# Whitening in place: output tiles written where their input tiles lay, and 26 instead of 21 tile places in SBUF

## The chip, the cores and the metric

One core of one Trainium2 chip. The time is that of one execution in device microseconds; of several executions the median is given. The profile is of one further execution. Engines are named TensorE (PE in the rows, its weight loads PEld), VectorE (DVE), ScalarE (ACT), GpSimd (POOL) and SyncE (SP), whose queue issues every DMA of this kernel. One core has 16 DMA engines.

## What is computed

Two layers on x of shape (4, 64, 256, 256), float32. First, each channel is convolved with a separable long filter (causal in both directions) and x times a bias is added. Then the result is whitened over channels:

```python
x1   = transpose(x, (1, 0, 2, 3)).reshape(64, -1)
x1_s = x1[:, ::9]                                   # every ninth position
mean = x1_s.mean(-1);  cov = x1_s @ x1_s.T / n + 0.01 * I
D    = isqrt_newton_schulz(cov, 5)                  # five Newton steps
out  = D @ (x1 - mean)                              # back to (4, 64, 256, 256)
```

The whole convolution must be done before the covariance is known, and the covariance before the first output.

## The kernel before

**Convolution.** 128 units (64 channels in each of two sweeps, two of the four images per sweep). For a unit, SP loads a tile of x (`x_sb`, five slots) and two Toeplitz tiles made from the filters (`hankel`), ScalarE and GpSimd split operands into a rounded high part and a rest (`rounded`), TensorE does two passes of matmuls (L633 to L636, `make_v`, `make_y`), VectorE adds bias times x into `y_sb` (L510, two slots), SP stores that to `y_dram` in HBM (`store_y`, two DMAs of 256 KB), GpSimd multiplies it by a mask of every ninth position into `masked` (L368), and VectorE sums that into `z_sb` (L518). TensorE is one unit ahead of the evictions.

**Join.** `z_sb` gives the covariance (`covariance`, 58 matmuls per sweep; that of the second sweep is what `cov_mm` 2 stands for). Then a chain of small operations between TensorE, VectorE and ScalarE makes `dmat` (the matrix D on 128 partitions, both image halves at once) and the mean's share in `small[:, 6:7]` (`d_ready`). Its small operands (`cov`, `sq`, `wm` and so on) lie in `z_all` behind the output slots, the constants `halves`, `ident15`, `ident_eps`, `twice` in the last x slot.

**Whitening.** 64 tiles of 128 x 2048 float32, 1 MB each (`TILES`, `TW`). A tile is loaded from `y_dram` to a place `t_in[t % slots]`, multiplied by `dmat` in four matmuls of 512 columns (L744; the profile has two records of each), the left half evicted from PSUM by ScalarE (L442) and the right half by VectorE (L613) into one of `O_SLOTS` = 4 output slots `t_out`, and stored to `out` (L287). ScalarE and VectorE wait until the store of tile t - 4 has landed. There are 21 places: 14 (`kept`) are loaded during the second sweep, three lie in `rounded`, one in `plain`, two in `x_all`, one in `y_all`; `z_all` and `masked_all` hold the output slots.

SP's queue is one order written out by hand. After the last unit: loads of tiles 14 to 17 (when TensorE has done its last convolution matmul, `y_mm`), `store_y(LAST)`, tiles 18 and 19, a wait for all stores of y (L299) and for the last masks and sums (`z_last_done`), tile 20. Then per tile t:

```python
while loaded < min(TILES, max(slots + t * 2 // 5, t + LEAD)):   # LEAD = 7
    sp.wait_ge(t_mm[1], loaded - slots + 1)                     # its place has been read
    load_tile(loaded)
    loaded += 1
sp.wait_ge(t_act, t + 1)
sp.wait_ge(t_dve, t + 1)                                        # L313
store_tile(t)
```

So two loads go out for every five tiles, until the lead of the loads has come down to 7 tiles; from then on one load per tile.

Of the kernel before, what the change touches and what calls it, by code (L numbers as in the profile page):

```python
# [13 lines left out]
P = 128  # L14
# [43 lines left out]
O_SLOTS = 4  # L58
# [4 lines left out]
def conv_whiten(nc, x, first, hidden, columns, bias, out):  # L63
# [3 lines left out]
    with ExitStack() as ctx:  # L67
# [8 lines left out]
        kept = sb("kept", [P, KEPT * TW])  # L76
# [13 lines left out]
        plain = sb("plain", [P, T_SLOTS * 2 * P + 2 * 2 * S + H_SLOTS * 2 * S])  # L90
# [7 lines left out]
        x_all = sb("x_all", [P, X_SLOTS * XW])  # L98
        x_sb = [x_all[:, k * XW:(k + 1) * XW] for k in range(X_SLOTS)]
        y_all = sb("y_all", [P, 2 * XW])  # L100
        y_sb = [y_all[:, k * XW:(k + 1) * XW] for k in range(2)]
        masked_all = sb("masked_all", [P, 2 * BLOCKS * GW])
        masked = [masked_all[:, k * BLOCKS * GW:(k + 1) * BLOCKS * GW].rearrange("p (i w) -> p i w", w=GW)
                  for k in range(2)]
        z_all = sb("z_all", [P, ZROWS * ZW])
        z_sb = z_all[:, :].rearrange("p (r m) -> p r m", m=ZW)
# [16 lines left out]

        o_cols = (O_SLOTS - 1) * TW
        cov, sq, t_even, t_odd, dmat, wm, mm_sq, zm = (z_all[:, o_cols + k * P:o_cols + (k + 1) * P] for k in range(8))
        tm = (t_even, t_odd)
        ident15, ident_eps, halves, twice = (x_sb[X_SLOTS - 1][:, k * P:(k + 1) * P] for k in range(4))

        t_in = [kept[:, k * TW:(k + 1) * TW] for k in range(KEPT)]
        t_in += [rounded[:, k * TW:(k + 1) * TW].bitcast(F32) for k in range(3)] + [plain[:, 0:TW]]  # L130
        after_v = len(t_in)
        t_in += [x_all[:, k * TW:(k + 1) * TW] for k in range(2)]
        after_y = len(t_in)
        t_in += [y_all[:, 0:TW]]
        slots = len(t_in)
        t_out = [z_all[:, k * TW:(k + 1) * TW] for k in range(O_SLOTS - 1)] + [masked_all[:, 0:TW]]

# [27 lines left out]
        t_loaded = [sem(f"t_loaded{k}") for k in range(slots)]  # L165
        t_mm = [sem(f"t_mm{u}") for u in range(2)]
        t_act, t_dve = sem("t_act"), sem("t_dve")
        t_stored = [sem(f"t_stored{k}") for k in range(O_SLOTS)]
# [32 lines left out]
        def _(sp):  # L201
# [81 lines left out]
            def load_tile(t):  # L283
                sp.dma_start(t_in[t % slots], tile_in(t, 0, TW)).then_inc(t_loaded[t % slots], 16)

            def store_tile(t):
                sp.dma_start(out[t], t_out[t % O_SLOTS]).then_inc(t_stored[t % O_SLOTS], 16)  # L287


            sp.wait_ge(y_mm, UNITS)  # L290
            for t in range(KEPT, after_v):
                load_tile(t)
            store_y(LAST)
            for t in range(after_v, after_y):
                load_tile(t)
            for k in range(2):
                sp.wait_ge(y_stored[k], 32 * (UNITS // 2))
            sp.wait_ge(masked_half, PER)
            sp.wait_ge(z_last_done, 2 * PER)  # L299
            for t in range(after_y, slots):  # L300
                load_tile(t)
# [476 lines left out]
```

## Time and profile before

| | |
|---|---|
| three runs | 954.18, 952.86, 945.55 us, median 952.86 |
| profiled execution | 948.63 us, span 946.5 us |
| granted TensorE clock, mean | 0.996 |
| busy: TensorE, weight loads, VectorE, ScalarE, GpSimd | 868.5, 729.9, 576.3, 401.0, 494.5 us |
| DMA | 306.36 MB, mean 324 GB/s |

The span runs from the first to the last instruction of the profiled execution; the execution's own time is 2.1 us longer. All times in the rows are microseconds from the start of the span, unless they are marked ns. The busy share of an engine over the whole span is an average over the three stages above; they have to be read apart.

### The profile page before, as it was taken

The page shows a single profiled execution, that of the slowest core. Times are in us where ns is not written, and L with a number is a line of the kernel's source. Part 1 is how long each engine was busy: PE and PEld are TensorE (multiplying, and loading weights), DVE is VectorE, ACT ScalarE, POOL GpSimd, SP SyncE. Part 2 cuts the span into 40 slices and gives each one's busy share as a digit, 9 for nine tenths or more (in the row PEclk, how much of TensorE's full clock was granted, in tenths as well). Part 3 has the DMA queues.
Part 4 walks back from the last instruction along what each step waited for, and adds up shares of the span by engine and source line. Part 5 has one row for each costly group of instructions (what it writes and reads, how often), then busy time and mean ns, then how long its engine had stood idle before and what let it go on. Part 6 is the DMA issues. An engine that isn't in the chain of part 4 may idle for free.

```text
span 946.5 us, 15709 instructions
## 1 busy us (share of the span) xinstructions
PE 868.5 (92%) x5970; PEld 729.9 (77%) x5970; DVE 576.3 (61%) x641; ACT 401.0 (42%) x715; POOL 494.5 (52%) x278
## 2 busy tenths in 40 slices
PE   2799999999999999999999999999999997777774
PEld 0799999999999999999999999999544442322221
DVE  5388787788888847878777878784333332222222
ACT  2355555555555525555555555550233322222221
POOL 2298888888888856878777778771000000000000
PEclk9999999999999999999999999999999999999998
DMA  2799998999999866999999999988499999999998
GB/s 105 218 315 293 284 283 276 297 278 291 279 287 287 283 218 194 341 335 339 329 343 332 357 334 330 340 279 331 170 413 422 421 423 427 427 427 427 427 428 360
DMA packets 99351, 306.36 MB, mean 324 GB/s; under 512 B 13484, under 2 KB 48333, under 8 KB 84685
## 3 DMA queue, kind: packets, MB, share of 16 engines
q1 hardware_dynamic: 99276, 305.37, 90.8%
q8 instruction: 47, 0.77, 0.3%
q14 instruction: 28, 0.22, 0.1%
HBM read 167.96 MB, written 137.36 MB: 323 GB/s over the span
## 4 chain that ended last, share of the span: by engine, by line
PE 77%; DMA 18%; DVE 3%; issue 1%; ACT 0%; SPq 0%; DVEq 0%; ACTq 0%
PE ps L636 24%; DMA out<-z_all 17%; PE ps L633 13%; PE ps L634 13%; PE ps L635 13%; PE ps L744 10%; PE ps L665 3%; DVE z_all L613 1%; DVE kept L470 1%; PE ps L684 0%; DMA plain<-filters 0%; PE ps L624 0%; ACT z_all L442 0%; DMA kept<-hidden 0%; PE ps L721 0%
## 5 line engine op out<-in xcount | busy, mean ns | idle before, releaser
L633 PE MATMUL ps<-rounded 128*128 128x256 f32 x1024 | 373.7, 365 | 10.3 <-DVE rounded L499 8.7
L368 POOL TENSOR_TENSOR masked_all<-y_all,mask 128x1024 f32<-128x1024 f32 x126 | 326.3, 2590 | 63.3 <-DVE y_all L510 63.1
L635 PE MATMUL ps<-rounded 128*128 128x256 f32 x1024 | 289.5, 283 | 0.0
L634 PE MATMUL ps<-rounded 128*128 128x256 f32 x1024 | 288.4, 282 | 0.0
L510 DVE SCALAR_TENSOR_TENSOR y_all<-x_all,bias_sb,ps 128x1024 f32<-128x1024 f32 x127 | 162.5, 1280 | 96.8 <-DMA convolved<-y_all 60.5
L334 POOL TENSOR_TENSOR rounded<-x_all,rounded 128x512 fp32r<-128x512 f32 x128 | 165.1, 1290 | 83.1 <-ACT rounded L401 82.5
L633 PEld LDWEIGHTS ps<-rounded 128*128 128x128 f32 x1024 | 196.5, 192 | 11.8 <-issue 11.4
L636 PE MATMUL ps<-plain,x_all 128*128 128x128 f32 x1024 | 197.4, 274 | 0.0
L634 PEld LDWEIGHTS ps<-rounded 128*128 128x128 f32 x1024 | 197.3, 193 | 0.0
L636 PE MATMUL ps<-plain 128*128 128x128 f32 x1024 | 196.4, 273 | 0.0
L635 PEld LDWEIGHTS ps<-rounded 128*128 128x128 f32 x1024 | 192.9, 188 | 0.0
L744 PE MATMUL ps<-kept,z_all 128*128 128x512 f32 x344 | 152.3, 596 | 22.2 <-ACT z_all L442 17.2
L636 PEld LDWEIGHTS ps<-plain,x_all 128*128 128x128 f32 x1024 | 159.0, 191 | 0.0
L636 PEld LDWEIGHTS ps<-plain 128*128 128x128 f32 x1024 | 158.0, 190 | 0.0
L518 DVE TENSOR_REDUCE z_all<-masked_all 128x116 f32<-128x1044 f32 x126 | 155.5, 1234 | 0.0
L744 PEld LDWEIGHTS ps<-kept,z_all 128*128 128x128 f32 x344 | 63.8, 190 | 109.7 <-issue 109.7
L613 DVE TENSOR_SCALAR z_all<-ps,small 128x1024 f32<-128x1024 f32 x48 | 61.6, 1284 | 140.6 <-PE ps L744 75.4
L408 ACT COPY plain<-ps 128x512 f32<-128x512 f32 x128 | 75.0, 586 | 156.1 <-PE ps L636 155.7
L442 ACT ACTIVATE z_all<-ps,small 128x1024 f32<-128x1024 f32 x48 | 53.4, 1113 | 157.2 <-DMA out<-z_all 102.9
L401 ACT CAST rounded<-x_all 128x512 fp32r<-128x512 f32 x128 | 80.2, 626 | 77.4 <-DMA x_all<-x 77.0
L490 DVE TENSOR_TENSOR rounded<-ps,rounded 128x512 fp32r<-128x512 f32 x128 | 87.9, 686 | 28.1 <-ACT rounded L410 27.9
L499 DVE TENSOR_TENSOR rounded<-plain,rounded 128x512 fp32r<-128x512 f32 x128 | 90.7, 709 | 13.4 <-ACT rounded L392 13.4
(103 smaller groups left out, 479.8 us busy)
## 6 DMA issues: line engine op xcount, KB each, us to landing
x_all<-x SPq DMA_DIRECT2D x128, 512.0 KB, 5.6
convolved<-y_all SPq DMA_DIRECT2D x256, 256.0 KB, 5.3
out<-z_all SPq DMA_DIRECT2D x48, 1024.0 KB, 15.7
plain<-filters SPq DMA_DIRECT2D x256, 128.0 KB, 4.8
kept<-convolved SPq DMA_DIRECT2D x29, 1024.0 KB, 19.9
out<-masked_all SPq DMA_DIRECT2D x16, 1024.0 KB, 15.2
kept<-convolved SPq DMA_DIRECT2D x28, 512.0 KB, 6.3
rounded<-convolved SPq DMA_DIRECT2D x9, 1024.0 KB, 20.2
```

Of the source, the lines that this page charges most:

```text
L334: nc.gpsimd.tensor_tensor(x_lo[k], row_block(q % X_SLOTS, 0), x_hi[k].bitcast(F32), ALU.subtract).then_inc(x_lo_done, 1)
L368: nc.gpsimd.tensor_tensor(masked_of(k, 0, PER), by_image(y_sb[k]), mask_of(q // C, 0, PER), ALU.mult).then_inc(masked_done, 1)
L401: nc.scalar.copy(x_hi[q % 2], row_block(k, 0)).then_inc(x_hi_done, 1)
L490: nc.vector.tensor_tensor(v_lo[k], ps_v[k][:, :, 0:S], v_hi[k].bitcast(F32), ALU.subtract).then_inc(v_lo_done, 1)
L499: nc.vector.tensor_tensor(t_lo[k], hankel[h][:, :, ::-1], t_hi[k].bitcast(F32), ALU.subtract).then_inc(t_lo_done, 1)
L510: nc.vector.scalar_tensor_tensor(y_sb[k], x_sb[q % X_SLOTS], bias_sb[:, q % C:q % C + 1], ps_y[k].rearrange("p a n -> p (a n)"), ALU.mult, ...
L518: nc.vector.tensor_reduce(z_of(q % C), grouped(q % 2, 0, BLOCKS), AX_X, ALU.add).then_inc(z_done, 1)
L633: mm(wide, hi[:, b, cols], t_hi[k][:, f, :], start=True, stop=False)
L634: mm(wide, hi[:, b, cols], t_lo[k][:, f, :], start=False, stop=False)
L635: mm(wide, lo[:, b, cols], t_hi[k][:, f, :], start=False, stop=False)
L636: last = mm(o[:, b, m * S + P:(m + 1) * S], block1[:, b, cols], t_f32[k][:, f, :], start=False, stop=True)
L744: last = mm(ps[:, bank(t, u) + r, :], dmat, t_in[k][:, w:w + IMG], start=True, stop=True)
```

## The change

All buffers of the convolution that are float32 now lie in one tensor `arena` of 24 tile widths: `kept`, `plain`, `x_all`, `y_all`, `z_all`, `masked_all`, in this order and without gaps. Whitening sees the same stretch as 23 places of one tile each, and three more in `rounded`, which are only read. The 24th tile width holds the small operands of the join. A tile's output is written where its input lay, half by half, once the matmuls of that half are done; the tiles in `rounded` (14, 15 and 16) write to the places of tiles 7, 8 and 9, whose stores they wait for. Output slots are gone. A load waits until the store of the tile that had its place has landed (it waited for matmuls before). Place and waits of every tile are worked out ahead, from a queue `free`.

SP's order after the last unit: tiles 14 to 18, `store_y(LAST)`, tiles 19 and 20, the wait for all stores of y and for the last masks, tile 21, waits for `z_last_done` and now also `cov_mm` 2, tiles 22 to 25. The loop then has 26 where it had 21. `halves` is set after a wait of GpSimd for `z_last_done`.

```diff
--- before.py
+++ after.py
@@ -55,7 +55,11 @@
 TILES = SWEEPS * SWEEP_TILES
 KEPT = 14
 PIECES = 2
-O_SLOTS = 4
+ARENA = 24 * TW
+READ_ONLY = 3
+OUT_OF = 7
 LEAD = 7
 MASK_COLS = 288
@@ -73,7 +77,14 @@
-        kept = sb("kept", [P, KEPT * TW])
+        arena = sb("arena", [P, ARENA])
+        taken = [0]
+        def region(cols):
+            taken[0] += cols
+            return arena[:, taken[0] - cols:taken[0]]
+        kept = region(KEPT * TW)
         rounded = sb("rounded", [P, 14 * 2 * S], F32R)
@@ -87,7 +98,7 @@
         v_hi = [rounded_at(10 + k, S) for k in range(2)]
         v_lo = [rounded_at(12 + k, S) for k in range(2)]
-        plain = sb("plain", [P, T_SLOTS * 2 * P + 2 * 2 * S + H_SLOTS * 2 * S])
+        plain = region(T_SLOTS * 2 * P + 2 * 2 * S + H_SLOTS * 2 * S)
         t_f32 = [plain[:, k * 2 * P:(k + 1) * 2 * P].rearrange("p (f n) -> p f n", n=P) for k in range(T_SLOTS)]
         at = T_SLOTS * 2 * P
         v_f32 = [plain[:, at + k * 2 * S:at + (k + 1) * 2 * S].rearrange("p (f n) -> p f n", n=S) for k in range(2)]
@@ -95,15 +106,15 @@
         hankel = [plain[:, at + k * 2 * S:at + (k + 1) * 2 * S].rearrange("p (f n) -> p f n", n=S)
                   for k in range(H_SLOTS)]
-        x_all = sb("x_all", [P, X_SLOTS * XW])
+        x_all = region(X_SLOTS * XW)
         x_sb = [x_all[:, k * XW:(k + 1) * XW] for k in range(X_SLOTS)]
-        y_all = sb("y_all", [P, 2 * XW])
+        y_all = region(2 * XW)
         y_sb = [y_all[:, k * XW:(k + 1) * XW] for k in range(2)]
-        masked_all = sb("masked_all", [P, 2 * BLOCKS * GW])
+        z_all = region(ZROWS * ZW)
+        z_sb = z_all[:, :].rearrange("p (r m) -> p r m", m=ZW)
+        masked_all = region(2 * BLOCKS * GW)
         masked = [masked_all[:, k * BLOCKS * GW:(k + 1) * BLOCKS * GW].rearrange("p (i w) -> p i w", w=GW)
                   for k in range(2)]
-        z_all = sb("z_all", [P, ZROWS * ZW])
-        z_sb = z_all[:, :].rearrange("p (r m) -> p r m", m=ZW)
         mask = sb("mask", [P, MASK_COLS])
@@ -121,19 +132,37 @@
         index, idx, near = (kept[:, 12 * S + k * MASK_COLS:12 * S + (k + 1) * MASK_COLS] for k in range(3))
-        o_cols = (O_SLOTS - 1) * TW
-        cov, sq, t_even, t_odd, dmat, wm, mm_sq, zm = (z_all[:, o_cols + k * P:o_cols + (k + 1) * P] for k in range(8))
+        in_place = ARENA // TW - 1
+        places = [arena[:, k * TW:(k + 1) * TW] for k in range(in_place)]
+        places += [rounded[:, k * TW:(k + 1) * TW].bitcast(F32) for k in range(READ_ONLY)]
+        resident = len(places)
+        after_v, after_x, after_y = KEPT + 2, KEPT + 4, KEPT + 5
+        in_at = [*range(KEPT), *range(in_place, resident), *range(KEPT, in_place)]
+        out_at, stores_of = [], [0] * in_place
+        stores_before_load, stores_before_out = [0] * resident, []
+        loads_of, loads_before = [0] * resident, []
+        free = []
+        for t in range(TILES):
+            if t >= resident:
+                in_at.append(free.pop(0))
+                stores_before_load.append(stores_of[in_at[t]])
+            k = in_at[t]
+            loads_of[k] += 1 if t >= KEPT else 0
+            loads_before.append(loads_of[k])
+            out_at.append(k if k < in_place else OUT_OF + k - in_place)
+            stores_before_out.append(0 if k < in_place else stores_of[out_at[t]])
+            stores_of[out_at[t]] += 1
+            if not OUT_OF <= t < OUT_OF + READ_ONLY:
+                free.append(out_at[t])
+        behind = [arena[:, in_place * TW + k * P:in_place * TW + (k + 1) * P] for k in range(TW // P)]
+        cov, sq, t_even, t_odd, dmat, wm, mm_sq, zm = behind[:8]
+        halves, ident15, ident_eps, twice = behind[12:]
         tm = (t_even, t_odd)
-        ident15, ident_eps, halves, twice = (x_sb[X_SLOTS - 1][:, k * P:(k + 1) * P] for k in range(4))
-        t_in = [kept[:, k * TW:(k + 1) * TW] for k in range(KEPT)]
-        t_in += [rounded[:, k * TW:(k + 1) * TW].bitcast(F32) for k in range(3)] + [plain[:, 0:TW]]
-        after_v = len(t_in)
-        t_in += [x_all[:, k * TW:(k + 1) * TW] for k in range(2)]
-        after_y = len(t_in)
-        t_in += [y_all[:, 0:TW]]
-        slots = len(t_in)
-        t_out = [z_all[:, k * TW:(k + 1) * TW] for k in range(O_SLOTS - 1)] + [masked_all[:, 0:TW]]
         ps = ctx.enter_context(nc.psum_tensor("ps", [P, 8, S * 2], F32))
         ps_v = [ps[:, 2 * k:2 * k + 2, :] for k in range(2)]
@@ -162,10 +191,10 @@
         t_ready, sq_mm, sq_copied = sem("t_ready"), sem("sq_mm"), sem("sq_copied")
         w_mm, w_copied, z_mm, z_copied = sem("w_mm"), sem("w_copied"), sem("z_mm"), sem("z_copied")
         d_made, mean_mm, d_ready = sem("d_made"), sem("mean_mm"), sem("d_ready")
-        t_loaded = [sem(f"t_loaded{k}") for k in range(slots)]
+        t_loaded = [sem(f"t_loaded{k}") for k in range(resident)]
-        t_stored = [sem(f"t_stored{k}") for k in range(O_SLOTS)]
+        t_stored = [sem(f"t_stored{k}") for k in range(in_place)]
         def wait(eng, s, value):
             if value > 0:
@@ -281,39 +310,42 @@
                 load_kept(q)
             def load_tile(t):
-                sp.dma_start(t_in[t % slots], tile_in(t, 0, TW)).then_inc(t_loaded[t % slots], 16)
+                wait(sp, t_stored[out_at[t]], 16 * stores_before_load[t])
+                sp.dma_start(places[in_at[t]], tile_in(t, 0, TW)).then_inc(t_loaded[in_at[t]], 16)
             def store_tile(t):
-                sp.dma_start(out[t], t_out[t % O_SLOTS]).then_inc(t_stored[t % O_SLOTS], 16)
+                sp.dma_start(out[t], places[out_at[t]]).then_inc(t_stored[out_at[t]], 16)
             sp.wait_ge(y_mm, UNITS)
-            for t in range(KEPT, after_v):
+            for t in range(KEPT, after_v + READ_ONLY):
                 load_tile(t)
             store_y(LAST)
-            for t in range(after_v, after_y):
+            for t in range(after_v + READ_ONLY, after_x + READ_ONLY):
                 load_tile(t)
             for k in range(2):
                 sp.wait_ge(y_stored[k], 32 * (UNITS // 2))
             sp.wait_ge(masked_half, PER)
+            for t in range(after_x + READ_ONLY, after_y + READ_ONLY):
+                load_tile(t)
             sp.wait_ge(z_last_done, 2 * PER)
-            for t in range(after_y, slots):
+            sp.wait_ge(cov_mm, 2)
+            for t in range(after_y + READ_ONLY, resident):
                 load_tile(t)
-            loaded = slots
+            loaded = resident
             for t in range(TILES):
-                while loaded < min(TILES, max(slots + t * 2 // 5, t + LEAD)):
-                    sp.wait_ge(t_mm[1], loaded - slots + 1)
+                while loaded < min(TILES, max(resident + t * 2 // 5, t + LEAD)):
                     load_tile(loaded)
                     loaded += 1
                 sp.wait_ge(t_act, t + 1)
                 sp.wait_ge(t_dve, t + 1)
                 store_tile(t)
-            for k in range(O_SLOTS):
-                sp.wait_ge(t_stored[k], 16 * (TILES // O_SLOTS))
+            for k in range(in_place):
+                sp.wait_ge(t_stored[k], 16 * stores_of[k])
         @block.gpsimd
         def _(pool):
@@ -377,6 +409,7 @@
             chained(nc.gpsimd.tensor_scalar(ident_eps, ident[:], EPS, None, ALU.mult))
             for k in range(2):
                 nc.gpsimd.tensor_tensor(twice[:, k * C:(k + 1) * C], ident[:, 0:C], ident[:, C:P], ALU.add)
+            pool.wait_ge(z_last_done, 2 * PER)
             nc.gpsimd.memset(halves, 0.5).then_inc(ident_ready, 1)
         @block.scalar
@@ -437,9 +470,9 @@
             for t in range(TILES):
                 act.wait_ge(t_mm[0], t + 1)
-                wait(act, t_stored[t % O_SLOTS], 16 * (t // O_SLOTS))
+                wait(act, t_stored[out_at[t]], 16 * stores_before_out[t])
                 src = ps[:, bank(t, 0):bank(t, 0) + 2, :].rearrange("p r n -> p (r n)")
-                nc.scalar.activation(t_out[t % O_SLOTS][:, 0:TW // 2], src, ACT.Identity,
+                nc.scalar.activation(places[out_at[t]][:, 0:TW // 2], src, ACT.Identity,
                                      bias=small[:, 6:7]).then_inc(t_act, 1)
         @block.vector
@@ -608,9 +641,9 @@
             for t in range(TILES):
                 dve.wait_ge(t_mm[1], t + 1)
-                wait(dve, t_stored[t % O_SLOTS], 16 * (t // O_SLOTS))
+                wait(dve, t_stored[out_at[t]], 16 * stores_before_out[t])
                 src = ps[:, bank(t, 1):bank(t, 1) + 2, :].rearrange("p r n -> p (r n)")
-                nc.vector.tensor_scalar(t_out[t % O_SLOTS][:, TW // 2:TW], src, small[:, 6:7], None, ALU.add
+                nc.vector.tensor_scalar(places[out_at[t]][:, TW // 2:TW], src, small[:, 6:7], None, ALU.add
                                         ).then_inc(t_dve, 1)
         @block.tensor
@@ -730,9 +763,9 @@
             for t in range(TILES):
                 if t < KEPT:
                     pe.wait_ge(kept_loaded, 16 * KEPT * PIECES)
-                k = t % slots
-                wait(pe, t_loaded[k], 16 * (t // slots + (1 if k >= KEPT else 0)))
+                k = in_at[t]
+                wait(pe, t_loaded[k], 16 * loads_before[t])
                 if t == 1:
                     pe.wait_ge(d_ready, 1)
@@ -741,7 +774,7 @@
                     wait(pe, t_dve if u else t_act, t - 1)
                     for r in range(2):
                         w = (2 * u + r) * IMG
-                        last = mm(ps[:, bank(t, u) + r, :], dmat, t_in[k][:, w:w + IMG], start=True, stop=True)
+                        last = mm(ps[:, bank(t, u) + r, :], dmat, places[k][:, w:w + IMG], start=True, stop=True)
                     last.then_inc(t_mm[u], 1)
```

## Rows read from the trace of the kernel before

**Rows 1.** The page: 40 equal slices of the span, DMA share in tenths, bytes per second.

```profile
DMA  2799998999999866999999999988499999999998
GB/s 105 218 315 293 284 283 276 297 278 291 279 287 287 283 218 194 341 335 339 329 343 332 357 334 330 340 279 331 170 413 422 421 423 427 427 427 427 427 428 360
```

**Rows 2.** The chain that ended last, 640 to 946 us, longest pieces: start, length, what.

```profile
669.42 85.96 PE ps L744 x200
...
873.89 18.17 DMA out<-z_all
```

**Rows 3.** Waits, 664 to 946 us: engine line, released by: total us, times, longest.

```profile
ACT z_all L442 <- DMA out<-z_all: 102.9, 28, 3.8
...
DVE z_all L613 <- DMA out<-z_all: 65.1, 19, 3.6
...
ACT masked_all L442 <- DMA out<-masked_all: 34.6, 10, 3.8
...
DVE masked_all L613 <- DMA out<-masked_all: 21.7, 6, 3.6
```

**Rows 4.** Stretches: length, each engine, granted clock, DMA share, GB/s.

```profile
652.00:656.00 4.00, 4.00 (x38) 4.00 (x38) 0.00 (x0) 0.00 (x0) 0.00 (x0) 1.00 1.02 378
...
664.00:674.40 10.40, 10.08 (x46) 6.37 (x46) 4.09 (x12) 1.11 (x1) 0.00 (x0) 1.00 0.04 14
674.40:684.00 9.60, 9.60 (x24) 4.22 (x23) 3.27 (x3) 3.34 (x3) 0.00 (x0) 1.00 0.74 300
684.00:700.00 16.00, 16.00 (x39) 7.15 (x38) 5.72 (x5) 5.57 (x5) 0.00 (x0) 1.00 1.00 383
700.00:755.00 55.00, 55.00 (x130) 24.35 (x129) 20.54 (x16) 17.37 (x16) 0.00 (x0) 1.00 1.01 422
755.00:930.00 175.00, 136.80 (x303) 54.66 (x302) 47.51 (x37) 40.52 (x37) 0.00 (x0) 1.00 1.01 426
930.00:941.00 11.00, 5.08 (x12) 1.78 (x10) 3.85 (x3) 3.34 (x3) 0.00 (x0) 0.91 1.01 428
941.00:944.00 3.00, 0.00 (x0) 0.00 (x0) 0.00 (x0) 0.00 (x0) 0.00 (x0) 0.50 0.55 232
944.00:946.50 2.50, 0.00 (x0) 0.00 (x0) 0.00 (x0) 0.00 (x0) 0.00 (x0) 0.50 0.06 26
```

**Rows 5.** SP's queue in order of time: start, duration of the issues, DMAs.

```profile
641.19 2.12 SPq L284 DMA_DIRECT2D rounded<-convolved  x3
643.35 1.41 SPq L284 DMA_DIRECT2D plain<-convolved  x1
645.53 1.25 SPq L242 DMA_DIRECT2D convolved<-y_all  x2
646.83 1.06 SPq L284 DMA_DIRECT2D x_all<-convolved  x2
659.09 0.32 SPq L284 DMA_DIRECT2D y_all<-convolved  x1
674.43 7.13 SPq L287 DMA_DIRECT2D out<-z_all  x3
681.61 0.42 SPq L284 DMA_DIRECT2D kept<-convolved  x1
```

**Rows 6.** TensorE in order of time: the second covariance.

```profile
644.27 13.19 PE L665 MATMUL ps<-z_all 128*128 128x129 f32 x116 [1.14 <-DVE z_all L548]
```

**Rows 7.** GpSimd in order of time, inside the convolution (idle before in brackets).

```profile
301.75 2.77 POOL L368 TENSOR_TENSOR masked_all<-y_all,mask 128x1024 f32<-128x1024 f32 x1 [0.62 <-DVE y_all L510]
304.49 1.28 POOL L334 TENSOR_TENSOR rounded<-x_all,rounded 128x512 fp32r<-128x512 f32 x1
306.38 2.78 POOL L368 TENSOR_TENSOR masked_all<-y_all,mask 128x1024 f32<-128x1024 f32 x1 [0.62 <-DVE y_all L510]
```

**Rows 8.** DMA issues, 640 to 700, then 700 to 946 us: median us to landing.

```profile
out<-z_all SPq DMA_DIRECT2D x6, 1024.0 KB, 5.8
...
out<-z_all SPq DMA_DIRECT2D x42, 1024.0 KB, 18.1
```

## The prediction

> **What bounds the kernel now.** I read the page's 40 slices first. The DMA row is at 9 nearly everywhere from the second slice on, falls to 4 in the slice from 662 to 686 us (the 29th) and is then 9 to the end, while GB/s goes from about 280 to 340 in the convolution to about 425 behind it [rows 1]. So there are three stages with different limits: the convolution (TensorE has no gap in it), a short join of covariance and Newton steps, and whitening. The chain of waits says what sets the end of the last: one piece of 86 us of TensorE (L744, 200 matmul records, 0.43 us each, so 3.43 us for the eight records of a tile), and from 755 us on stretches of 18.2 us of an output's transfer with one short eviction between them [rows 2]. The waits give the same from the other side: ScalarE waited 102.9 + 34.6 us and VectorE 65.1 + 21.7 us until an output tile had left its slot [rows 3]. That looks like a shortage of output slots, which is just what this change removes. The stretches show that it isn't one: from 755 to 930 us the DMA engines are at 1.01 and move 426 GB/s, no less than anywhere else in the trace [rows 4]. A slot comes free late because the transfers before it fill all sixteen engines. In whitening the time is the number of bytes divided by 426 GB/s, plus the time in which those engines stand still.
>
> They stand still once: 0.04 busy from 664.0 to 674.4 and 0.74 from 674.4 to 684.0, so 10.0 + 2.5 = 12.5 us idle [rows 4]. SP's queue says why. After the last matmul of the convolution it issues four loads, the last unit's two stores, two more loads, one at 659.09, and then nothing until the first output at 674.43: all 21 places are taken [rows 5].
>
> **The change part by part.** *Bytes.* The same 64 tiles are loaded once and stored once, 1.0486 MB each; one such transfer is 1.0486 MB / 426 GB/s = 2.46 us. Nothing is removed from the bytes.
>
> *Five more loads ahead of the first output.* With 26 places instead of 21, five loads (5 x 2.46 = 12.3 us) go ahead of tile 0. When? Five (not four) are issued once the last matmul is done, then the last unit's stores, then two. The next waits for those stores. Before, they had landed at 659.09 [rows 5]; one load more stands ahead of them, so 661.5. The queue then still holds what it held before (it ran dry at 664 with the load of 659.09 in it, so at 661.5 without, plus 2.46 us for the fifth: 664.0), a margin of 2.5 us. The four last places need the second covariance as well (the new wait on cov_mm), whose matmuls end at 644.27 + 13.19 = 657.46 [rows 6]: earlier, so this wait ends nothing. The five loads thus run from 664.0 to 676.3, of which 10.4 us lie in the hole and 1.9 us run on past the first store's issue at 674.43. Stores come every 3.43 us there (three issues in 7.13 us [rows 5]) and take 2.46 us, so the hole's tail takes these up; but between second and third store some 0.8 us stay idle because the third isn't computed yet. Of 12.5 us idle, 12.5 - 0.8 = 11.7 us are filled.
>
> *Is a filled hole time saved?* Only if a queue stands behind it. Until the loads catch up, one store and 0.4 load per tile cost 1.4 x 2.46 = 3.44 us of DMA for 3.43 us of TensorE: balanced, no backlog, TensorE ends last. The loop goes over to one load per tile where 21 + 0.4t falls below t + 7, at t = 24 (751 us, and the chain turns to DMA at 755 [rows 2]); with 26 it is t = 32. So eight tiles, 27 us, move from the DMA-bound rate to the balanced one, which shows 422 instead of 426 GB/s [rows 4]: 0.3 us lost. Behind t = 32 the DMA has 4.92 us of work per tile against TensorE's 3.43, a backlog grows by 1.49 us a tile, and everything saved ahead of it is saved at the end: 11.7 - 0.3 = 11.4 us.
>
> *Waits of ScalarE and VectorE on output slots.* These 224 us of waiting vanish, since an output has its input's place; only tiles 14, 15 and 16 wait, for the stores of tiles 7, 8 and 9, issued 24 us earlier. Worth nothing by itself: what is late next is the load. LEAD is still 7, so once TensorE has run ahead it stops for the load of its own tile, behind about six loads and six stores, 12 x 2.46 = 29.5 us. Expect TensorE waiting for DMA where it waited for ScalarE. At the end the last load has some five stores queued behind it (12.3 us) and the last tiles need 3.43 + 1.3 us, so the DMA stays full. Before it was full there too: 1.01 up to 941, then 0.55 and 0.06 [rows 4], so nothing is won at the tail.
>
> *Load waits at the head of SP's queue.* The load of tile n now waits for the landed store of an earlier tile, where it waited for matmuls. The stores that follow stand behind it in that queue. The tight one is the first, load 26 at t = 3, which needs store 0. That one starts at 676.3, ends at 678.8; the first six outputs took 5.8 us to land (the median), with a short queue, which with 1.9 us for the spill is 682.1 [rows 8], against an SP that came there at 681.61 [rows 5]: about 0.5 us of waiting, with a store still in the queue. Next comes store 1 at t = 5, 3.4 us later relative to need, and from n = 33 on the distance is 23 to 24 tiles. I take zero. Upper bound: a store lands as late as 12.3 us after issue, as the last unit's two did (issued by 646.8, landed 659.09, with two loads behind them [rows 5]); SP would then stand until 686.7 and the fourth output go out 2 us late. Loss 2 to 5 us, no gain possible.
>
> *Small things.* `halves` now waits on GpSimd for z_last_done, ahead of 657.46, and is read after it: nothing. Of 23 final waits instead of four, at most 8 follow the last landing, 0.05 us each at the "issue" pieces' size: 0.2 us, taken as 0.2.
>
> *Layout of the convolution's buffers.* No instruction is added in 128 units. The trace can't show the new addresses. GpSimd is the engine with least room: product 2.78 us, difference 1.28 us, idle 0.62 us, in a unit of 4.63 us [rows 7]. The two products shown write different halves of masked_all, 4,176 bytes apart, and take 2.77 and 2.78 us; so I price another address at nothing. The Trainium skill (SBUF — State Buffer, Door 1: the DMA port swizzle) says that lines of SBUF are 16 bytes and each crossing to a new one costs; masked_all now begins at byte 186,600 of the stretch, 8 past such a line, one line more per row of 1,024 bytes. That would be at most 1 part in 64 of 2.78 us, 0.04 us, inside the idle; the sum is the same by it.
>
> Sum: 11.4 - 0.2 = 11.2 us off the profiled execution, 948.6 - 11.2 = 937.4 (span 946.5 to 935.3). The median of the three runs shown is 952.9 and gives 941.7; the three runs and the profiled one have a mean of 950.3 and give 939.1. I say 940.
>
> The Trainium skill speaks against the rate on which all this rests: DMA: Bandwidth & Descriptors (Where 436 GB/s comes from) has transfers between HBM and SBUF bound by some 358 GB/s per core. By it a transfer would take 2.93 us and five of them 14.6 us, 2.2 us more than the hole holds. The trace disagrees, with 426 GB/s over 175 us [rows 4].
>
> **The rivals.** *The deeper queue moves fewer bytes per second (slower).* Before, an output took 18.1 us to land [rows 8], so 18.1 / 2.46 = 7.4 transfers were in flight, held there by four output slots. After, nothing holds it but LEAD: up to 12. If reads and writes then disturb each other in HBM, each per cent costs 2.5 us of the 102 transfers (251 us). The gain is gone at 405 GB/s, and the kernel is over 1% slower below 391. At the 378 GB/s of 652 to 656 us, the lowest busy rate of this stage [rows 4], the 102 transfers take 283 us, 32 us more: 940 + 32 = 972. For it: that stretch had a full queue. Against it: the last unit's 64-partition stores were in it, and from 3 in flight (422) to 7 (426) the rate rose.
>
> *The convolution becomes GpSimd's.* If other addresses lengthen the product at L368 beyond its 0.62 us of idle, all 127 units pay. At +0.83 us (30%) it is 0.21 x 127 = 27 us: 940 + 27 = 967. Over 1% slower from +0.80 us on. Against it, the equal pair of products.
>
> *Part of the hole stays.* SP stands at its new head waits (2 to 5 us lost as above), or the last unit's stores land later than 664.0 and the five loads start late. Gain 3 to 9 us: 941 to 948, likeliest 945. For it: one-load margins of 2.5 us.
>
> *More than the hole.* Without the lockstep of slots the DMA could hold the 428 GB/s of 930 to 941 us [rows 4], or up to 1% more, throughout: another 1.2 to 2.5 us, and starts between engines even out: 935 to 938.
>
> *The change doesn't do what it says* in one respect: the three places in `rounded` are only read once, so 23 serve again and again. With LEAD at 7 that costs nothing, and has no case of its own.
>
> **How the numbers follow.** Hole filled, 936 to 944: 0.63. More than the hole, 931 to 938: 0.13. Part of it stays: 0.14. Slower rate: 0.06. GpSimd: 0.04. Repeats of the kernel before differ by 8.6 us, so about 1% is what a measurement can tell; I add 4 us at each end. The range is 931 to 950: it leaves out the two slow cases and the edges of the others. Faster by over 1% needs 9.5 us, close to the 11.2: nine tenths of the first case, the second and little of the third, 0.69; within 1%: 0.22; slower by over 1%: 0.09.
>
> **What the profile after would show.** The DMA share at 664 to 674 near 1 instead of 0.04; five loads issued between about 661 and 664; tile 0 still at 669. No waits of ScalarE or VectorE for outputs, TensorE waiting for loads late in the stage, the chain on TensorE for some 50 tiles and then on loads. Landing times of outputs up to 25 or 30 us at an unchanged 426 GB/s: if this falls, the first rival holds. If GpSimd's L368 is longer, the second. If SP waits long for outputs near 682, the third. My prediction fails if a filled hole brings a new one later: look for any DMA share below 1 between 684 and the end.

## The result: 1.1% less, as much as the idle time that was filled

Over 20 runs each, the changed kernel takes 939.5 us in the median (937.1 to 950.2) and the kernel before 952.5 us; the ratio is 0.9888, interval 0.9868 to 0.9908. Ratios here compare fast runs alone (one of the kernel before, 1009.4 us, was slow) and are not the quotients of the medians, which is 0.986 for this pair. The profiled execution took 937.1 us, its span is 934.9 us (948.6 and 946.5 before). It has 11.6 us less, and the sum above had 11.2.

Read the 40 slices of the page of the changed kernel first, beside those of [rows 1]. The slice with 4 tenths and 170 GB/s is gone; what follows is the same.

```profile
DMA  3799999999989984999999999997999999999998
GB/s 106 242 305 287 282 284 285 283 281 287 288 278 296 285 256 150 348 342 321 358 345 314 323 331 353 344 325 256 407 381 422 423 424 422 426 427 427 427 427 342
```

The stretches of the changed kernel (length, each engine, granted clock, DMA share, GB/s) answer to [rows 4]. The share at 664 to 674 us is 1.01, where it was 0.04. From 674 to 684 us it is 0.94, where it was 0.74. From 790 us on the rate is 427 GB/s, with more transfers in flight than before.

```profile
660.00:664.00 4.00, 3.68 (x27) 3.09 (x27) 2.10 (x9) 0.19 (x1) 0.00 (x0) 1.00 1.01 422
664.00:674.20 10.20, 9.88 (x44) 6.11 (x43) 4.09 (x12) 1.11 (x1) 0.00 (x0) 1.00 1.01 424
674.20:684.00 9.80, 9.80 (x24) 4.37 (x23) 3.53 (x3) 3.34 (x3) 0.00 (x0) 1.00 0.94 379
684.00:700.00 16.00, 16.00 (x38) 7.03 (x37) 5.46 (x5) 5.57 (x5) 0.00 (x0) 1.00 0.99 386
700.00:790.00 90.00, 90.00 (x211) 39.90 (x210) 33.91 (x27) 28.94 (x26) 0.00 (x0) 1.00 1.01 423
790.00:926.00 136.00, 104.87 (x231) 41.69 (x229) 37.99 (x30) 32.28 (x29) 0.00 (x0) 1.00 1.01 427
```

SP's queue in order of time, against [rows 5]. The five loads went out from 660.16 to 662.38, with the queue still busy; the first output followed at 674.17, within 0.3 us of its old time.

```profile
643.09 1.90 SPq L314 DMA_DIRECT2D arena<-convolved  x2
645.33 1.10 SPq L271 DMA_DIRECT2D convolved<-arena  x2
...
660.16 2.22 SPq L314 DMA_DIRECT2D arena<-convolved  x5
```

The waits from 664 us on answer to [rows 3]. No wait of ScalarE or VectorE for an output transfer is left; TensorE's records wait for loads instead, 25.6 us, and the evictions wait for TensorE.

```profile
ACT arena L475 <- PE ps L777: 188.5, 64, 10.9
DVE arena L646 <- PE ps L777: 170.3, 64, 3.7
...
PE ps L777 <- DMA arena<-convolved: 25.6, 22, 1.2
```

The chain of waits answers to [rows 2]: TensorE sets the end until 803 us, then the loads do.

```profile
669.16 134.02 PE ps L777 x312
...
804.95 23.49 DMA arena<-convolved
828.49 2.00 PE ps L777 x4
832.37 25.51 DMA arena<-convolved
```

### The profile page after: what moved, and what is told of

Its sections match the earlier page's. It is cut to its first block, busy times and chain, and to the rows that moved or that the text cites. A ratio compares the mean times of both kernels' runs of the same rounds, so it can differ in the third digit from the quotient of the medians.

```text
span 934.9 us, 15604 instructions
## 1 busy us (share of the span) xinstructions
PE 865.4 (93%) x5970; PEld 729.6 (78%) x5970; DVE 577.7 (62%) x641; ACT 401.6 (43%) x715; POOL 494.3 (53%) x278
## 4 chain that ended last, share of the span: by engine, by line
PE 83%; DMA 12%; DVE 2%; issue 1%; ACT 1%; SPq 0%; DVEq 0%
PE ps L669 24%; PE ps L777 15%; PE ps L666 13%; PE ps L667 13%; PE ps L668 13%; DMA arena<-convolved 11%; PE ps L698 3%; DVE arena L503 1%; PE ps L717 0%; DMA arena<-filters 0%; ACT arena L475 0%; DVE arena L646 0%; PE ps L657 0%; SPq L317 0%; DMA arena<-hidden 0%
## 5 line engine op out<-in xcount | busy, mean ns | idle before, releaser
L669 PE MATMUL ps<-arena 128*128 128x128 f32 x2048 | 393.8, 274 | 0.0
L400 POOL TENSOR_TENSOR arena<-arena,mask 128x1024 f32<-128x1024 f32 x126 | 325.7, 2585 | 69.1 <-DVE arena L543 68.8
L669 PEld LDWEIGHTS ps<-arena 128*128 128x128 f32 x2048 | 315.9, 190 | 0.0
L777 PE MATMUL ps<-arena 128*128 128x512 f32 x488 | 215.7, 597 | 25.6 <-DMA arena<-convolved 25.6
L543 DVE SCALAR_TENSOR_TENSOR arena<-arena,bias_sb,ps 128x1024 f32<-128x1024 f32 x127 | 162.6, 1280 | 91.3 <-PE ps L669 45.8
L777 PEld LDWEIGHTS ps<-arena 128*128 128x128 f32 x488 | 90.8, 190 | 149.5 <-issue 105.7
L366 POOL TENSOR_TENSOR rounded<-arena,rounded 128x512 fp32r<-128x512 f32 x128 | 165.2, 1291 | 77.3 <-ACT rounded L434 76.6
L646 DVE TENSOR_SCALAR arena<-ps,small 128x1024 f32<-128x1024 f32 x64 | 82.2, 1284 | 170.3 <-PE ps L777 170.3
L551 DVE TENSOR_REDUCE arena<-arena 128x116 f32<-128x1044 f32 x126 | 155.5, 1234 | 0.0
L434 ACT CAST rounded<-arena 128x512 fp32r<-128x512 f32 x128 | 80.5, 629 | 45.7 <-DMA arena<-x 45.4
L532 DVE TENSOR_TENSOR rounded<-arena,rounded 128x512 fp32r<-128x512 f32 x128 | 89.7, 701 | 12.5 <-ACT rounded L425 12.4
L425 ACT CAST rounded<-arena 128x512 fp32r<-128x512 f32 x128 | 78.9, 617 | 0.0
```

The costliest lines, as they stand in the source:

```text
L366: nc.gpsimd.tensor_tensor(x_lo[k], row_block(q % X_SLOTS, 0), x_hi[k].bitcast(F32), ALU.subtract).then_inc(x_lo_done, 1)
L400: nc.gpsimd.tensor_tensor(masked_of(k, 0, PER), by_image(y_sb[k]), mask_of(q // C, 0, PER), ALU.mult).then_inc(masked_done, 1)
L532: nc.vector.tensor_tensor(t_lo[k], hankel[h][:, :, ::-1], t_hi[k].bitcast(F32), ALU.subtract).then_inc(t_lo_done, 1)
L543: nc.vector.scalar_tensor_tensor(y_sb[k], x_sb[q % X_SLOTS], bias_sb[:, q % C:q % C + 1], ps_y[k].rearrange("p a n -> p (a n)"), ALU.mult, ...
L551: nc.vector.tensor_reduce(z_of(q % C), grouped(q % 2, 0, BLOCKS), AX_X, ALU.add).then_inc(z_done, 1)
L646: nc.vector.tensor_scalar(places[out_at[t]][:, TW // 2:TW], src, small[:, 6:7], None, ALU.add).then_inc(t_dve, 1)
```

## Experiments

The theory under test: whitening lasts as long as its bytes take at the full rate, plus the time in which the DMA engines have nothing to do. The change moved five transfers into such a time, and that is the whole gain. The main rival: output slots were short, and writing in place is what pays. All variants are edits of the changed kernel unless said otherwise. In the table "whitening" is the time from the issue of the first output to the end of the span, in the one profiled execution; "fall" is how long the DMA engines took from full rate (above 350 GB/s) to the last of them finishing, read in slices of 0.3 us. The variants ran in four groups, each beside the kernel before on the same chip, whose medians there were 950.8 (e1 to e4), 949.5 (e5 to e8), 950.7 (e9 to e11) and 950.7 us (e12); across groups the ratios are to be compared, not the medians. The convolution ahead of it varies by a few microseconds between executions of one kernel (in one profile, the repeat of 1/2, by 11 us), so that whitening is compared by this column.

| kernel | median us | ratio to before | whitening us | fall us |
|---|---|---|---|---|
| before | 952.5 | 1 | 272.1 | 4.2 |
| changed | 939.5 | 0.9888 (0.9868 to 0.9908) | 260.7 | 4.2 |
| changed, repeated (e5_after) | 939.4 | 0.9882 (0.9857 to 0.9906) | 263.2 | 7.2 |
| 21 ahead (e1_early21) | 951.4 | 1.0002 (0.9977 to 1.0028) | 270.7 | 2.1 |
| 23 ahead (e2_early23) | 946.0 | 0.9949 (0.9927 to 0.9971) | 270.8 | 7.2 |
| four slots' waits (e3_lock4) | 941.2 | 0.9902 (0.9874 to 0.9929) | 264.0 | 4.5 |
| pace 1/2 (e4_cad_half) | 935.7 | 0.9835 (0.9806 to 0.9864) | 258.5 | 2.7 |
| pace 1/2, repeated (e6_cad_half_again) | 934.7 | 0.9843 (0.9814 to 0.9873) | 258.5 | 2.7 |
| pace 3/5 (e7_cad_3of5) | 936.8 | 0.9844 (0.9815 to 0.9873) | 258.5 | 2.7 |
| lead 14 (e8_lead14) | 938.2 | 0.9871 (0.9846 to 0.9897) | 262.2 | 6.3 |
| lead 5 (e9_lead5) | 938.2 | 0.9870 (0.9831 to 0.9908) | 263.7 | 3.3 |
| before, pace 1/2 (e10_before_half) | 949.6 | 0.9991 (0.9960 to 1.0022) | 274.1 | 4.5 |
| pace 1/2, lead 5 (e11_half_lead5) | 935.2 | 0.9828 (0.9791 to 0.9866) | 258.7 | 3.0 |
| pace 1/3 (e12_third) | 942.9 | 0.9908 (0.9872 to 0.9944) | 266.1 | 6.0 |

### How many loads go ahead

```diff
+EARLY = 21          # e2_early23: 23
-            for t in range(after_x + READ_ONLY, after_y + READ_ONLY):
+            for t in range(after_x + READ_ONLY, min(EARLY, after_y + READ_ONLY)):
...
-            for t in range(after_y + READ_ONLY, resident):
+            for t in range(after_y + READ_ONLY, EARLY):
...
-            loaded = resident
+            loaded = EARLY
             for t in range(TILES):
-                while loaded < min(TILES, max(resident + t * 2 // 5, t + LEAD)):
+                while loaded < min(TILES, max(EARLY + t * 2 // 5, t + LEAD)):
```

> The changed kernel with outputs in place and no output slots, but only 21 tiles loaded ahead of tile 0, as many as before; the other five are loaded in the loop at the pace of before. Theory (the gain is the five transfers moved into the DMA engines' idle time ahead of the first output, 5 x 2.46 us, and the vanished waits for output slots are worth nothing): the gain is gone, ratio to the kernel before 0.998 to 1.003; DMA share near 0.04 again between 664 and 674 us; span 946 to 948. Rival (the slots were short, in place is what pays): it stays near 0.989, about 941 us.

> The same with 23 tiles ahead of tile 0. Theory: two of five transfers are moved, 2 x 2.46 = 4.9 us, ratio 0.993 to 0.997, span about 941. Rival (slots): as the changed kernel, 0.989.

With 21 ahead the ratio is 1.0002: everything of the change is still in the kernel (in place, no slots, 26 places) except the five early transfers, and the gain is gone (the span is 948.9 us, 946 to 948 were expected). The stretch of 10 us ahead of its first output (the convolution ended later in this execution, so it lies at 668 to 678 us) stands idle as before:

```profile
668.20:678.20 10.00, 9.68 (x43) 5.93 (x42) 3.91 (x12) 1.11 (x1) 0.00 (x0) 1.00 0.01 6
```

With 23 ahead, two transfers are worth 1 - 0.9949 = 0.5%, 950.8 - 946.0 = 4.8 us in the medians of that chip, where 4.9 was expected. Its one trace doesn't show it: whitening is 270.8 us there beside 270.7 with 21 ahead, since a fall longer by 5.1 us takes up what two transfers give, and its span is 944.6 us where 941 was expected. More on the fall below. So the dose of two rests on the medians (the interval leaves out both 1 and 0.989). The rival falls with 21 ahead alone.

### The waits of four output slots, put back

```diff
+SLOTS = 4
...
                 wait(act, t_stored[out_at[t]], 16 * stores_before_out[t])
+                if t >= SLOTS:
+                    wait(act, t_stored[out_at[t - SLOTS]], 16 * stored_with[t - SLOTS])
```

The same stands on VectorE; `stored_with[t]` (its lines are left out here) is how many stores the place of tile t has had, tile t's among them.

> The changed kernel with all 26 tiles ahead of tile 0, in place, but ScalarE and VectorE wait for the landed store of tile t - 4 before they evict tile t, as with four output slots. Theory: the waits for outputs come back (over 150 us of ScalarE) and the time stays, ratio to before 0.987 to 0.991, span 934 to 936. Rival (slots): it goes back towards the kernel before, 0.997 to 1.0.

The waits came back in full, in its list of waits from 664 us on:

```profile
ACT arena L480 <- DMA out<-arena: 132.6, 40, 5.2
DVE arena L653 <- DMA out<-arena: 89.4, 27, 5.0
```

The time did not: 0.9902, interval 0.9874 to 0.9929, holds both ratios of the changed kernel. The trace does show a price, though, that the expectation had at zero. The engines run short near the end, 0.77 and 322 GB/s against 424 up to there, that is 8 x (1 - 322/427) = 2.0 us:

```profile
700.00:918.00 218.00, 188.13 (x426) 78.49 (x424) 66.75 (x52) 56.84 (x51) 0.00 (x0) 1.00 1.01 424
918.00:926.00 8.00, 5.49 (x13) 2.31 (x13) 3.18 (x3) 2.86 (x3) 0.00 (x0) 1.00 0.77 322
```

The span expected was 934 to 936 and is 938.5. So output slots are worth 0 to 2 us here, and at the end only. Even this can't be told apart from the uneven progress of the DMA engines, which was largest in this trace (8.2 us, see the next section).

### The pace of the loads

```diff
-                while loaded < min(TILES, max(resident + t * 2 // 5, t + LEAD)):
+                while loaded < min(TILES, max(resident + t // 2, t + LEAD)):
```

The variants have `t * 3 // 5` and `t // 3`; e10_before_half is the kernel before with `slots + t // 2`.

> The changed kernel with one load for every two tiles in the first part of the loop instead of two for five, so 1.5 instead of 1.4 transfers per tile: 3.69 us of DMA against 3.43 us of TensorE. Theory: DMA is the only limit of whitening, and its small shortfalls after tile 0 (386 GB/s from 684 to 700 us, 423 up to 790, against 427) are a queue that now and then runs empty. A queue that grows from the start takes up to 1.0 + 0.9 us of them: 0 to 3 us less than the changed kernel, ratio to before 0.986 to 0.989. Rival (the lower rate is the mix of loads and stores, or latency at the start): no difference to the changed kernel.

> The changed kernel as it is, beside the three that follow, to compare them on one chip. Ratio to the kernel before 0.987 to 0.991.

> The changed kernel with one load for two tiles (1.5 transfers per tile) once more, to see on one chip how far it is from the changed kernel. Theory (whitening is bytes over the full rate plus the time in which the queue runs empty; a growing queue covers the small shortfalls): 1 to 3 us under the changed kernel. Rival (the lower median of the first trial was the chip's or the runs' spread): within 1 us of it.

> Three loads for five tiles (1.6 transfers per tile, 3.94 us of DMA against 3.43 us of TensorE). Theory: the queue grows twice as fast, the shortfall after 700 us vanishes sooner, but most of it lies before 700 us where no place is free for an earlier load: as with 1.5, or at most 0.5 us less. If more transfers in flight cost rate, it is slower than with 1.5.

The changed kernel repeats at 0.9882. With 1.5 transfers per tile it is 934.7 beside 939.4 on the same chip, with 1.6 it is 936.8. That is 3 to 5 us, more than the 0 to 3 that missing rate could give: the expectations were too low, and the ratio of the first trial, 0.9835, is under the 0.986 to 0.989 given. The intervals of the two on one chip still overlap (0.9857 to 0.9906 and 0.9814 to 0.9873); that the pace acts rests on four sets of runs with at least 1.5 against four with 1.4, in times and traces alike. The traces say that rate is the smaller part. At the old pace 3.5 us are missing against 427 GB/s in the first 115 us of whitening (3.6 in the repeat), with 1.5 it is 2.9 us (2.7). The rest lies in the fall: the last 12.0 us move 3.10 MB in the changed kernel and 2.09 MB in its repeat, 3.61 to 3.73 MB in the four with at least 1.5. The DMA share of the last 12.0 us in 40 slices of 0.3 us, for the changed kernel, its repeat, and the first trial of pace 1/2, in this order:

```profile
DMA  9999999999999999999976433321111111000000
```

```profile
DMA  9999999999974333333222221111000000000000
```

```profile
DMA  9999999999999999999999999975343320000000
```

In the repeat the rate is off at 928 us and single engines work on until 936; with pace 1/2 all sixteen stop within 2.7 us. Three traces with at least 1.5 transfers per tile at lead 7, and a fourth at lead 5, have 258.5 to 258.7 us of whitening; those with 1.4, all 26 ahead and no slot waits have 260.7 to 263.7.

The traces also show when the engines come apart. Each DMA leaves sixteen completion marks, the last of which is its landing. If all engines were equally far on, the marks of one DMA would lie close together. The time from its first mark to its last, median of the DMAs that landed in each stretch after the first output:

| kernel | 40 to 60 us | 80 to 100 us | 120 to 140 us | last output |
|---|---|---|---|---|
| before | 1.6 | 4.5 | 4.5 | 4.5 |
| changed | 1.2 | 3.6 | 4.8 | 4.8 |
| changed, repeated | 3.5 | 5.2 | 7.4 | 7.4 |
| lead 14 | 3.7 | 6.3 | 6.3 | 6.3 |
| lead 5 | 3.9 | 6.6 | 7.5 | 3.4 |
| four slots' waits | 3.3 | 5.7 | 8.2 | 4.5 |
| pace 1/2 | 1.5 | 2.3 | 2.3 | 3.0 |
| pace 1/2, repeated | 2.5 | 2.7 | 2.8 | 3.0 |
| pace 3/5 | 2.7 | 2.7 | 2.7 | 3.2 |
| pace 1/2, lead 5 | 2.6 | 2.6 | 2.6 | 3.2 |
| before, pace 1/2 | 4.0 | 6.1 | 7.7 | 4.6 |

So the fall is not made at the end. The engines drift apart in the part of whitening where DMA and TensorE are in balance, and keep the distance once DMA alone sets the pace; at the end it comes due. In place and at 1.5 or 1.6 transfers per tile they hardly drift. Why is open. The pace alone isn't enough: with 21 ahead and the old pace the distance stays at 2.5 us, and the kernel before drifts to 7.7 us with pace 1/2.

> The kernel before, with its four output slots and 21 places, and one load for two tiles instead of two for five. If the pace of loads pays by itself (a queue that never runs empty after tile 0), it pays here too: 0.3 to 2 us less, ratio 0.998 to 1.0. If the 3 to 5 us of the in-place kernel with that pace are an affair of its deep queue and its end, nothing: 0.999 to 1.001.

> The changed kernel with one load for three tiles in the first part of the loop instead of two for five: 1.33 transfers per tile, 3.27 us of DMA against 3.43 us of TensorE, the other side of 1.5 and 1.6. The DMA engines then idle 0.16 us per tile until one load per tile begins at t = 29, 4 to 5 us in all. Theory (whitening is bytes over the full rate, plus the time in which the engines stand still, plus what they finish apart at the end): 3 to 5 us over the changed kernel, ratio to before 0.991 to 0.994, share about 0.96 and 405 to 410 GB/s from 700 to 770 us. Rival (the pace acts only through how evenly the engines finish, and the rate before it isn't a limit): as the changed kernel, 0.987 to 0.990, with an uneven end.

In the kernel before the pace shows no effect (0.9991), but the interval, 0.9960 to 1.0022, holds both expectations and leaves room for 2 to 4 us either way. In the other direction, 1.33 transfers per tile take 942.9 us, 3.5 us over the changed kernel in the median, inside the 3 to 5 expected. The ratio of 0.9908 lies just below the 0.991 given, and its interval, 0.9872 to 0.9944, holds that of the changed kernel, so the time alone doesn't settle it. The rate does: in the stretch below 70 x (1 - 404/427) = 3.8 us are missing, in 90 us of the changed kernel 90 x (1 - 423/427) = 0.8 us. One expectation failed in an instructive way: the share was to fall to 0.96 and stayed at 1.01, while the rate fell to 404 GB/s, close to the 405 to 410 foretold:

```profile
700.00:770.00 70.00, 70.00 (x164) 30.97 (x163) 26.62 (x21) 22.26 (x20) 0.00 (x0) 1.00 1.01 404
```

A share of 1.01 is thus no proof that no more bytes could be moved. The GB/s are.

### The depth of the queue

```diff
-LEAD = 7
+LEAD = 14           # e9_lead5 and e11_half_lead5: 5
```

> The changed kernel with a lead of 14 tiles for the loads instead of 7; it goes over to one load per tile at t = 20 instead of 32. It tells how deep the queue can be and what depth costs. In the changed kernel the issues of SP took 0.33 to 0.5 us until 811 us and some 2 us each from then on, where TensorE began to wait for loads. Theory A (a full queue holds SP back at some 8 to 10 transfers in flight, and depth costs no rate): the long issues begin earlier, near tile 30, the landing time of a load stays at some 25 us, the rate at 427 GB/s, the time is that of the changed kernel or up to 2 us less. Theory B (deeper queues slow HBM): landing times well over 25 us, a rate under 420 GB/s, and a time over that of the changed kernel.

> The changed kernel with a lead of 5 tiles instead of 7: at most some five loads and five stores are wanted at once, so SP's queue should hardly fill. Open since the earlier runs: with 1.5 and 1.6 transfers per tile the kernel was 3 to 5 us faster than as changed, but only some 0.4 us of that is rate; the rest is in the last 8 us, where the share of the DMA engines falls evenly and late (two traces) instead of early and with a long tail of one to four engines (after and its repeat, lead 14, 23 ahead). Theory 1 (the uneven end comes from a full queue that holds SP back): no issue of SP over 1.5 us, a short tail, 2 to 4 us under the changed kernel. Theory 2 (it has nothing to do with the full queue): the tail stays, and the time is that of the changed kernel, 0.987 to 0.990, or a little above it.

> In place, one load for two tiles, lead 5. Theory 1: both are ways to the same short tail, so as with either alone, ratio 0.983 to 0.986. Theory 2: the pace alone acts, so as with one load for two tiles at lead 7, 0.983 to 0.986 too, if five tiles of lead keep the DMA full; under 0.3 us of rate lost.

In the changed kernel SP's own issues begin to last some 2 us at 812 us, and 34 of them take over 1.5 us from there on; in the whitening of the kernel before none does. Its queue around that time:

```profile
808.00 0.33 SPq L317 DMA_DIRECT2D out<-arena  x1
808.38 0.61 SPq L314 DMA_DIRECT2D arena<-convolved  x1
811.43 1.34 SPq L317 DMA_DIRECT2D out<-arena  x1
812.82 1.93 SPq L314 DMA_DIRECT2D arena<-convolved  x1
814.87 2.05 SPq L317 DMA_DIRECT2D out<-arena  x1
```

With a lead of 14 they begin at 767 us, near tile 28. Stores take 26.7 us to land in the median, loads 26.8 (issues from 780 to 900 us):

```profile
out<-arena SPq DMA_DIRECT2D x29, 1024.0 KB, 26.7
arena<-convolved SPq DMA_DIRECT2D x20, 1024.0 KB, 26.8
```

26.8 / 2.46 is 11 transfers, though twice the lead was asked for: SP is held back at about that depth, and the rate stays at 427 GB/s (0.9871, theory A). The deeper queue costs nothing. That also answers the first rival of the prediction, as far as it can be asked.

Lead 5 takes the long issues away altogether, and the kernel is no faster (938.2). With pace 1/2 it is as fast as pace 1/2 is alone (935.2). So Theory 1, that a full queue makes the uneven end, is refuted: the marks of a DMA come 7.9 us apart without one long issue, and the pace acts without a full queue. The fall of 3.3 us in the table says nothing against this, since the engines that are ahead wait in a gap before it. This gap is what an engine that lags costs. The last 12.0 us:

```profile
DMA  9999989732122227999989992110000000000000
```

The load of the last tile has its first mark at 914.6 and landed at 922.6, and by 926 most engines had done all that was queued. From 926 to 928 only one to three in ten are at work; the last output was issued at 927.7. Had the load not waited for its slowest engine, this gap would be shorter; with lead 7 two more loads and stores stand in the queue there, which I take to cover it.

## Why the prediction was right

*Bytes and rate.* Right. 2.46 us per transfer held at every depth up to 11. Five, none and two transfers ahead gave 11.6 us in the traces (11.2 foreseen), nothing, and 4.8 us in the medians (4.9 expected). That 11.2 and 11.6 are so close is partly luck: the repeat of the changed kernel, with a fall of 7.2 us, has a span of 937.1 us, 9.4 less than before.

*The five loads in the hole.* Right in place and time. Foreseen from 664.0, ahead of a queue that runs dry; issued from 660.16 on, when the last unit's stores had landed 1.3 us earlier than I had them. The wait on cov_mm ended nothing. 0.8 us of idle time between second and third store was foreseen; 674.2 to 684.0 us shows 0.94, so 0.6 us, or 1.1 us by its 379 GB/s against 427.

*Balanced part at 422 GB/s.* 423. The 0.3 us for eight more such tiles can't be told from the spread.

*Waits of ScalarE and VectorE worth nothing.* Right for the result; e3_lock4 puts their price at 0 to 2 us, not at none.

*What comes late next.* The engine and the cause were right (TensorE for its load), the place was not. I had the chain on TensorE for some 50 tiles; it is there for 134 us, 39 tiles. TensorE first stops at 813.74, (813.74 - 669.16) / 3.43 = tile 42. The step that failed took the 29.5 us of a full queue as the moment of the first stop. But a load goes out only six tiles ahead, 6 x 3.43 = 20.6 us, so TensorE stops as soon as a load takes longer than that; from then on loads took 25.5 us in the chain, 25.5 / 2.46 = 10 transfers rather than 12, since SP was held back in its issues. As the DMA engines stayed full, neither moved the end.

*Head waits of SP.* Right at zero: no wait of SP for an output is in its list before the last outputs.

*The tail.* "Nothing is won at the tail" was right for the one profiled execution (4.2 us of fall in both). That it can differ by 3 us between two traces of one kernel (4.2 and 7.2), and that pace moves it, I had not seen, although it is as large as a quarter of the gain.

*Small things.* Mis-sized, at no cost to the whole. From the last landing to the end of the span 0.96 us pass in every in-place trace, 0.47 in the kernel before: the longer list of final waits costs 0.5 us, where I had 0.2.

*Convolution and layout.* Right. Over the whole convolution GpSimd's product takes 2.61 us in the median (2.00 to 2.86) at its new addresses and 2.62 (2.01 to 2.84) before. The reason I gave was weak: the two halves of `masked_all` lie 4,176 = 261 x 16 bytes apart, so both lie alike to the 16-byte lines that the prediction goes by, and their equal times said nothing about a start 8 bytes past one. Two rows against [rows 7]:

```profile
300.49 2.78 POOL L400 TENSOR_TENSOR arena<-arena,mask 128x1024 f32<-128x1024 f32 x1 [0.58 <-DVE arena L543]
303.24 1.29 POOL L366 TENSOR_TENSOR rounded<-arena,rounded 128x512 fp32r<-128x512 f32 x1
```

Of the Trainium skill's rules, the one on a cost per line of SBUF crossed (SBUF — State Buffer, Door 1: the DMA port swizzle) gave an estimate of 0.04 us at most, and the trace shows none. The Trainium skill's limit of some 358 GB/s between HBM and SBUF (DMA: Bandwidth & Descriptors, Where 436 GB/s comes from) didn't bind this core, the only one at work: it moved 427 GB/s over 136 us.

## What to carry to other kernels

Where a stage is bound by DMA, look for the time ahead of it in which the DMA engines stand still, and count how many transfers fit: memory is worth just that many transfers, here 2.46 us a megabyte. That it is worth no more once the hole is full follows from the same account; no run had more than 26 places. Long waits for output slots are no argument for more slots while the rate behind them is the full one; put the waits back in an experiment and see. And try a pace of prefetches a little over the balance, not at it: here one line (1.5 instead of 1.4 transfers per tile) gave the in-place kernel another 0.4 to 0.5%, the best version of this study at 935 us. In the kernel before no such gain shows, and the cause is open, so measure it.

## What the runs showed of the hardware

SP's queue takes DMAs of 1 MB with little delay while at most nine before them haven't landed: most issues last 0.3 to 0.6 us and none in whitening over 1.8. With ten, an issue lasts 2.0 to 2.1 us in the median, in all nine traces that got there, and the landing time stays near 25 to 27 us, with lead 7 as with lead 14; no issue found more than eleven that hadn't landed. Up to there neither reads nor writes lost any rate (426 GB/s at 7.4 in flight, 427 at 10).

The share of the DMA engines reads 1.01 at 404 GB/s just as at 427.

The sixteen engines don't finish together. From full rate to the last one, 2.1 to 7.2 us passed. In the four traces in place with at least 1.5 transfers per tile it was 2.7 to 3.0 us, in the others in place 2.1 (21 ahead) to 7.2, and the long falls go with the longer whitening. They come apart while DMA and TensorE are in balance (from 1.2 to 4.8 us in the changed kernel) and keep their distance (4.8 us to the end) once DMA alone sets the pace. Why a queue that grows from the start keeps them together in place is open: the full queue isn't the cause (lead 5), and the completion marks don't say which engine lags.
